# Moving one stream's layer norm to another place in a software-pipelined attention kernel, on GpSimd, VectorE, ScalarE and SyncE

## The reference

```python
def block(h, p):
    r = _retention(h, wk)                       # q k^T, causal mask, row scale, times v
    a, gate = jnp.split(r @ w1 + b1, 2, axis=-1)
    m = a * jax.nn.silu(gate) @ w2 + b2
    y = _groupnorm1(m, gg, gb) + h              # one mean and variance for a whole sequence
    f = jax.nn.gelu(y @ wf1 + bf1_, approximate=False) @ wf2 + bf2_
    return (_layernorm(f + y, lg, lb), None)    # mean and variance of each token
x = _layernorm(x + scan(block))
x = _layernorm(x + experts(x))                  # gates = entmax_bisect(x Wr + br)
```

## Time and profile before

| | |
|---|---|
| Median of 3 runs | 2443.53 us (2442.73 to 2443.81) |
| The profiled execution | 2442.89 us, of which the span of its instructions is 2441.2 |
| PE busy | 2378.8 us, 97% |
| VectorE busy | 1606.4 us, 66% |
| GpSimd busy | 1433.5 us, 59% |
| ScalarE busy | 1341.2 us, 55% |
| One step (window 644 to 709 us of the span) | 65.0 us: PE busy 62.56, VectorE 47.27, ScalarE 41.28, GpSimd 36.75 |

### The profile page before, as it was taken

How to read it: one execution, slowest core, us unless ns; L and a number is a source line. 1 busy time by engine, 2 the same in 40 slices (tenths; PEclk the granted TensorE clock), 3 DMA queues, 4 the chain that set the end, 5 groups by cost and what they waited for, 6 DMA issues and landing times. The chain is left out here.

```text
span 2441.2 us, 34911 instructions
## 1 busy us (share of the span) xinstructions
PE 2378.8 (97%) x11242; PEld 1968.7 (81%) x11242; DVE 1606.4 (66%) x2953; ACT 1341.2 (55%) x2343; POOL 1433.5 (59%) x1565
## 2 busy tenths in 40 slices
PE   9999999999999999989999999999999999999998
PEld 7888778877888888777888888888888888888886
DVE  3667767667776776678887856665646756565545
ACT  5666666666666666655655544444444444444443
POOL 2345665566655755577987955555645556554444
PEclk9999999999999999999999999999999999999999
DMA  7134454443444344436756554543445433444442
GB/s 250 44 87 103 104 143 100 104 96 99 109 99 97 87 95 100 114 103 208 238 204 211 185 210 160 186 150 137 151 178 185 160 143 138 158 160 168 151 159 74
DMA packets 354870, 344.70 MB, mean 141 GB/s; under 512 B 233872, under 2 KB 319120, under 8 KB 338320
## 3 DMA queue, kind: packets, MB, share of 16 engines
q1 hardware_dynamic: 353728, 341.85, 45.0%
q10 hardware_dynamic: 976, 0.81, 0.1%
HBM read 244.70 MB, written 97.91 MB: 140 GB/s over the span
## 5 line engine op out<-in xcount | busy, mean ns | idle before, releaser
L808 POOL TENSOR_TENSOR hid_lo<-full,hid_hi 128x512 fp32r<-128x512 f32 x384 | 505.4, 1331 | 513.7 <-ACT full L1084 462.2
L1594 DVE SCALAR_TENSOR_TENSOR full<-ps,bias_cols,sum 128x512 f32<-128x512 f32 x384 | 288.1, 750 | 215.7 <-PE ps L1872 196.6
L1870 PE MATMUL ps<-hid_hi,m_w 128*128 128x512 f32 x1024 | 401.8, 392 | 0.1
L1872 PE MATMUL ps<-hid_hi,m_w 128*128 128x512 f32 x1024 | 398.8, 389 | 0.0
L1871 PE MATMUL ps<-hid_lo,m_w 128*128 128x512 f32 x1024 | 398.5, 389 | 0.0
L1081 ACT ACTIVATE hid_hi<-ps,bias_cols 128x512 fp32r<-128x512 f32 x128 | 88.3, 690 | 495.2 <-PE ps L1872 495.2
L1870 PE MATMUL ps<-te_hi,m_w 128*128 128x512 f32 x896 | 351.1, 392 | 1.6 <-DVE sum L1581 1.0
L1872 PE MATMUL ps<-te_hi,m_w 128*128 128x512 f32 x896 | 349.0, 390 | 0.0
L1871 PE MATMUL ps<-te_lo,m_w 128*128 128x512 f32 x896 | 348.7, 389 | 0.0
L1872 PEld LDWEIGHTS ps<-hid_hi,m_w 128*128 128x128 f32 x1024 | 192.2, 188 | 40.3
L1870 PEld LDWEIGHTS ps<-hid_hi,m_w 128*128 128x128 f32 x1024 | 192.3, 188 | 39.6 <-issue 0.5
(11 more groups left out here) (209 smaller groups left out, 5576.5 us busy)
## 6 DMA issues: line engine op xcount, KB each, us to landing
m_w<-prepared SPq DMA_DIRECT2D x96, 1408.0 KB, 6.0
prepared<-m_w SPq DMA_DIRECT2D x32, 1408.0 KB, 5.8
h_store<-h_out SPq DMA_DIRECT2D x32, 512.0 KB, 3.6
we_raw<-in_W SPq DMA_DIRECT2D x64, 256.0 KB, 6.4
gate_bc<-gate_rows SPq DMA_DIRECT2D x64, 256.0 KB, 6.3
z_store<-tmp SPq DMA_DIRECT2D x120, 128.0 KB, 4.0
z<-z_store SPq DMA_DIRECT2D x30, 512.0 KB, 3.9
hT_store<-z SPq DMA_DIRECT2D x96, 128.0 KB, 3.4
```

What stands on the lines that cost most here:

```text
L808: nc.gpsimd.tensor_tensor(out=hid_lo[:, k, :], in0=full[:, k, :], in1=f32(hid_hi[:, k, :]), op=ALU.subtract).then_inc(hid_ready, 1)
L1594: nc.vector.scalar_tensor_tensor(out=full[:, k, :], in0=src, scalar=b1_col(e, 2 * fp + BLOCK_ROW[k]), in1=other[:, :], op0=ALU.add, op1=AL ...
L1870: nc.tensor.matmul(out, w[0], x[0], start=first, stop=False, skip_group_check=True)
L1872: return nc.tensor.matmul(out, w[1], x[0], start=False, stop=last, skip_group_check=True)
```

## The change

It moves steps of B's layer norm and what lies around it; no arithmetic is added or left out.

- SyncE: B's store of z is issued by chunk (store_z_chunk), four transfers of 64 KB for c = 0 and four for c = 1, each behind its own turn_z. load_T(B) goes behind load_z(B). The counts Z_STORE and Z_MOVE become one for each slot.
- GpSimd: layernorm_rstd(B, earlier) goes to the head of the body (behind the split of qk at a seam); layernorm_out(B, earlier), eight instructions in one stretch, goes from behind rstd_group(A) and the split of f2 to behind split_f(B) and layernorm_rstd(A).
- ScalarE: normalise_z(B, earlier) goes behind high_t(A), in front of the scores of A; high_t(B) goes in front of the load of the Gelu table; the high half of vm at a seam goes in front of high_u(B, 1).
- VectorE: statistics and variance of B(earlier) go to the head of the body, in front of residual(A); turn_z(A) goes into the gated products of B, turn_h(A) behind them; statistics of A go in front of its gated products; residual(B, 0) goes between gated(A, 1) and low_u(A, 1), turn_z(B, 0) behind low_t(B), residual(B, 1) between groupnorm_var(A) and groupnorm_out(A), turn_z(B, 1) behind low_p(B), turn_h(B) directly behind it; in A's groupnorm_out summed(1) comes before low_y(0).
- TensorE: group_moments of B goes behind two blocks of A's scores instead of three, group_moments of A in front of the last quarter of down_projection(B, 1).

```diff
-        Z_STORE, Z_MOVE = P // BLOCK * DMA, (P // BLOCK + 1) * DMA
+        Z_STORE = [n * (P // BLOCK) * DMA for n in (1, DC)]
+        Z_MOVE = [n + DMA for n in Z_STORE]
...
+            def store_z_chunk(s, it, c):
+                sp.wait_ge(z_ready[s], it * U + residuals(s, c) + 1)
+                for q in range(P // BLOCK):
+                    sp.dma_start(z_blocks[s, q][:, c], turned_z(s)[q * BLOCK:(q + 1) * BLOCK, c, :].rearrange("p (n b) -> p n b", b=BLOCK)
+                                 ).then_inc(z_moved[s], DMA)
...
-                store_z(B_, it - 1)
+                for c in range(DC):
+                    store_z_chunk(B_, it - 1, c)
                 if lc_of is not None:
                     load_lc(B_, lc_of)
-                load_T(B_, it + 1)
                 if earlier and turn:
                     store_hT(B_, it - 2)
                 load_z(B_, it - 1, turn)
+                load_T(B_, it + 1)
...
@@ gpsimd body
+                if earlier:
+                    layernorm_rstd(B_, earlier)
                 split_h(A_, now)
...
                     split_f(B_, before)
+                    layernorm_rstd(A_, before)
                     if earlier:
-                        layernorm_rstd(B_, earlier)
-                    layernorm_rstd(A_, before)
+                        layernorm_out(pool, nc.gpsimd, B_, earlier)
...
                     split_weight("f2", now.layer)
-                if earlier:
-                    pool.wait_ge(y_ready[A_], now.base + 2)
-                    layernorm_out(pool, nc.gpsimd, B_, earlier)
...
@@ scalar body
                     gate(B_, before, 1)
+                    if seam:
+                        next_high_weight("vm", now.layer, m_psum[B_], before)
                     high_u(B_, before, 1)
                     load_table(ACT.Gelu)
                 high_t(A_, now)
-                if seam:
-                    next_high_weight("vm", now.layer, m_psum[B_], before)
+                if earlier:
+                    normalise_z(B_, earlier)
...
+                high_t(B_, now)
                 load_table(ACT.Gelu)
-                high_t(B_, now)
                 if before:
                     normalise_z(A_, before)
...
-                if earlier:
-                    normalise_z(B_, earlier)
...
@@ vector, groupnorm_out
                 summed(0)
-                between()
                 gained(1)
-                meanwhile(0)
-                low_y(s, at, 0)
-                meanwhile(1)
-                dve.wait_ge(gn_done[s], base + 10)
-                summed(1)
+                if s == A_:
+                    dve.wait_ge(gn_done[s], base + 10)
+                    summed(1)
+                    low_y(s, at, 0)
+                else:
+                    meanwhile(0)
+                    low_y(s, at, 0)
+                    meanwhile(1)
+                    dve.wait_ge(gn_done[s], base + 10)
+                    summed(1)
                 low_y(s, at, 1)
...
@@ vector body
+                if earlier:
+                    for blocks in HALVES:
+                        layernorm_stats(B_, earlier, blocks)
+                    layernorm_var(B_, earlier)
                 if before:
                     for c in range(DC):
                         residual(A_, before, c)
-                    for c in range(DC):
-                        turn_z(A_, before, c)
+                    gated_products(B_, before, lambda c: turn_z(A_, before, c))
                     if earlier and turn:
                         turn_h(A_, earlier)
-                    gated_products(B_, before)
...
-                if earlier:
+                if before:
                     for blocks in HALVES:
-                        layernorm_stats(B_, earlier, blocks)
-                    layernorm_var(B_, earlier)
+                        layernorm_stats(A_, before, blocks)
+                    layernorm_var(A_, before)
+                gated(A_, now, 0)
+                low_u(A_, now, 0)
+                gated(A_, now, 1)
                 if before:
-                    gated_products(A_, now, lambda part: layernorm_stats(A_, before, HALVES[part]))
-                    layernorm_var(A_, before)
                     residual(B_, before, 0)
-                    turn_z(B_, before, 0)
-                else:
-                    gated_products(A_, now)
+                low_u(A_, now, 1)
...
                 if before:
+                    turn_z(B_, before, 0)
                     groupnorm_in(A_, now)
                     groupnorm_var(A_, now)
-                groupnorm_out(A_, now, between=lambda: before and residual(B_, before, 1))
+                    residual(B_, before, 1)
+                groupnorm_out(A_, now)
+                low_p(B_, now, range(TB))
                 if before:
                     turn_z(B_, before, 1)
-                low_p(B_, now, range(TB))
+                if earlier and turn:
+                    turn_h(B_, earlier)
...
@@ tensor body
-                scores(A_, now, (0, 1, 2), before)
+                scores(A_, now, (0, 1), before)
                 if before:
                     group_moments(B_, before)
-                scores(A_, now, (3,), before)
+                scores(A_, now, (2, 3), before)
...
                     out_projection(A_, now)
-                    down_projection(B_, before, 1)
+                    down_projection(B_, before, 1, (0, 1, 2))
                 group_moments(A_, now)
-                if not before:
+                if before:
+                    down_projection(B_, before, 1, (3,))
+                else:
```

More of the change, by code:

```diff
@@ L527, in store_z @@
                                  ).then_inc(z_moved[s], DMA)
+            def store_z_chunk(s, it, c):
[3 more added lines that the diff above has]
+                                 ).then_inc(z_moved[s], DMA)
             def load_z(s, it, turned=True):
-                sp.wait_ge(z_moved[s], it * Z_MOVE + Z_MOVE + Z_STORE)
+                sp.wait_ge(z_moved[s], it * Z_MOVE[s] + Z_MOVE[s] + Z_STORE[s])
                 if turned:
@@ L615, in _ @@
                 sp.sem_inc(hT_stored[s], H_STORE)
-                sp.sem_inc(z_moved[s], Z_MOVE)
+                sp.sem_inc(z_moved[s], Z_MOVE[s])
             load_part(0, 0, kq_loaded)
@@ L670, in _ @@
             store_h(B_, STEPS - 3)
-            store_z(B_, STEPS - 2)
+            for c in range(DC):
+                store_z_chunk(B_, STEPS - 2, c)
             load_z(B_, STEPS - 2, False)
@@ L1321, in gated @@
                 if c == 0:
-                    dve.wait_ge(z_moved[s], at.it * Z_MOVE + Z_STORE)
+                    dve.wait_ge(z_moved[s], at.it * Z_MOVE[s] + Z_STORE[s])
                 dve.wait_ge(m_psum[s], at.base + 2 * c + 2)
@@ L1367, in groupnorm_var, with groupnorm_out @@
                                                op0=ALU.mult, op1=ALU.subtract, reverse1=True).then_inc(g_var[s], U)
-            def groupnorm_out(s, at, meanwhile=lambda part: None, between=lambda: None):
+            def groupnorm_out(s, at, meanwhile=lambda part: None):
                 sq, mom, rstd, gain, off0, off = group_parts(s)
@@ L1422, in layernorm_stats @@
                 else:
-                    dve.wait_ge(z_moved[s], at.it * Z_MOVE + 2 * Z_MOVE)
+                    dve.wait_ge(z_moved[s], at.it * Z_MOVE[s] + 2 * Z_MOVE[s])
                 for k in blocks:
@@ L1738, in body @@
                     low_hT(A_, step_behind(dve, now))
-                if earlier and turn:
-                    turn_h(B_, earlier)
                 for half in range(2):
```

## The result

The changed kernel takes 2405.77 us (median of 4 runs, 2404.53 to 2407.02) against 2443.13 us for the kernel before beside it: 0.9848 of it, 95% interval 0.9831 to 0.9865, 37.4 us less. The forecast was 2414, its range 2396 to 2436. The profiled execution took 2406.80 us, its span is 2405.1.

The account below looks back on a forecast made before the run. TensorE, busy for 97% of the span, was taken as the bound, so only its idle time could be won. 45.6 us gross less 4 and 12 gave 29.6 off 2442.9, plus 0.6 between profiled run and median: 2414, range 2396 to 2436.

Parts of the forecast that it names:

- The sum: Whole kernel: 45.6 us gross won, less 4 for A's moments and 12 for the step's head, 29.6 net.
- That term, 2.0 each: First steps of three layers: residual wait of 2.41 us goes, stall reappears at y(A); 2.0 us won each, 6 together.
- The head: Head of the step: z(B) lands 1.8 us late, TensorE loses 1.0 us with refilling, 12 us in 12 steps.
- The moments of A: A's moments, asked for before down_projection(B, 1) ends: wait of 0 to 0.9 us, 0.3 taken for 14 steps, 4 us.
- (1): Ordinary step, B's score block 3: TensorE's 0.92 us wait for residual(B, 1) goes, 1.1 us won.
- (2): Ordinary step: TensorE's 0.80 us wait for the low half of y(A), c = 1, goes, 1.0 us won.
- (3): Ordinary step: TensorE's two 0.27 us waits for GpSimd's low halves of f(A) go, 1.1 us won.
- (a): Rival: all covers hold, z(B) and gn_in arrive in time; 2398 us, chance 0.25.
- (c): Rival: GpSimd's norm beside low_u(A) delays out_projection(A), 7 us on top, 2421 us; counted within the forecast's chance of 0.43.
- (d): Rival, head: half transfers cost whole ones, z(B) 5.5 us late, 56 us lost in 12 steps; 2458 us, chance 0.10.
- (b): Rival, head of the step: z(B) 3 us late, 2.2 us of wait in 12 steps; 2428 us, chance 0.14.
- (e): Rival: waits go but work is bound one instruction later everywhere, y_hi(A) only 0.2 us ahead; 2441 us, chance 0.08.

Follow-up runs that it names:

- e3_resid_first: The changed kernel with A's two residuals in front of B's statistics at the head of VectorE's body; 2396.0 us, ratio 0.9811.
- e1_a_order: The kernel before with only A's order changed (residual(B, 1), summed(1) and A's moments earlier), B's norm left in place; 2441.7 us, ratio 0.9998.
- e2_norm_only: The changed kernel with A's old order put back, so B's layer norm stays moved; 2426.01 us, ratio 0.9933.
- e4_whole_store: The changed kernel with B's z stored in one piece again, four transfers of 128 KB; 2423.32 us, ratio 0.9925.
- e6_seam_split: On e3_resid_first, B's norm cut in two on GpSimd in a layer's first step, bias behind A's power; 2399.0 us, ratio 0.9819.

## Why the prediction was right, and where it was not

**The sum.** 45.6 gross, 12 for the head, 4 for the moments, 29.6 net; 37.4 measured. Ordinary intervals gained 2.1 us each on average (14.6 / 7), where 3.3 less 1.0 and 0.3 is 2.0; they are 61.3 to 63.8 us long, 62.7 on average, where 62.5 to 63.3 was written. The missing part lies in the first steps of the layers: 14.0 us for the six intervals around them, where the prediction's terms give some 9 (for each interval behind a first step 2.0 less 1.0 for the head, for each one before it 3.3 less 1.3). The interval behind a first step lost 3.0 to 3.6 us, since a stall of 2.41 us for the residual fell to 1.05 for y and 1.17 for gin. That term, 2.0 each, was sized too small. Apart, the three intervals behind a first step give 9.7 us where the terms say 3.0, and the three before one 4.3 where they say 6.0.

The traces show two things that the prediction had no term for. One is a single stall in the interval into the third layer's first step, in which TensorE, VectorE and ScalarE wait for nothing that the profile names. On TensorE it has grown from 0.95 to 2.37 us, and that interval gained only 0.7 us, the others of its kind 1.7 and 1.9. What causes it stays open. The line of the kernel before, then that of the changed one:

```profile
530.93 0.49 PE L1870 MATMUL ps<-ry_sp,w_fold 128*128 128x512 f32 x1 [0.95 <-issue]
...
514.90 0.49 PE L1885 MATMUL ps<-ry_sp,w_fold 128*128 128x512 f32 x1 [2.37 <-issue]
```

The other is TensorE's clock. In the kernel before its granted clock is 0.50 (1.2 GHz instead of 2.4) for 3.4 us from 317.3, for 6.8 us from 842.9 and for 6.8 us from 1078.4; the first two stretches lie at the end of, or just behind, a wait of 2.4 us for the residual (the third such wait, at 580.80, has none). In the changed kernel it is 0.50 for 3.4 us from 516.3, just behind the stall, and for 6.8 us from 1042.0. Matmuls of 512 columns start 0.43 us apart there instead of 0.23. That is 17.0 against 10.2 us. An estimate from the spacing gives at most 3 us of the 37.4, and less where a slower TensorE meets the next wait later: the intervals behind the first steps took 66.73, 66.78 and 67.03 us in the kernel before, with 3.4, 0 and 6.8 us at the lower clock, and only the second has a wait for y's low half (1.07 us).

**The head.** "z lands at 662.7: 1.8 us late": 1.75 in the step shown and 1.35 on average. The chain from store to load was priced at 8.6 us; it takes 8.60 in the step shown and 8.0 on average, 7.6 to 8.8. 0.8 us of wait for TensorE was foreseen at out_projection(B); it is there in eight steps, 0.28 to 1.05 us. e3_resid_first gives 9 us for what was priced at 12. This step holds, a little oversized. One figure beside it is a slip: with 12.5 us from store to landing for 0.8 of wait, a wait of 3.5 needs some 15 us and not 14.4.

**The moments of A.** "A wait between 0 and 0.9, mostly once. I take 0.3 for 14 steps." Wrong in place. In ordinary steps A's moments cause no wait to speak of; nine of the 13 waits for gin are at B's moments, which the change also asks for earlier (eight of 0.16 to 0.21 us and one of 0.45), and four at A's: three of 1.0 to 1.17 us in the first steps of a layer and one of 0.23. The total, 5.5 us, is near the 4 priced, by luck.

**The waits (1), (2) and (3) as separate terms.** This is the step that failed, though it does not show in the time. The prediction added the three waits as if each could be won without the others; it named what GpSimd slows as a part of (2) and gave that no share. The expectations of e1 and e2 took it at its word, (1) and (2) for the order and (3) for the norm: 2.1 and 1.1 us a step. e1_a_order wins 1 us and not 29, e2_norm_only 17 and not 5 to 12. In its place: (2) has two sufficient cures. GpSimd's norm slowed a sum from 0.74 to 1.22 us and a subtraction from 0.69 to 1.13, and with it gone the wait goes in the old order as well; the new order alone takes it away too. And neither (1) nor (2) can be won while the norm stands between y(A) and the masks: TensorE then reaches retain(B) before GpSimd. The forecast of the whole came out since the change does both; a forecast of either half by the same sum would have been off by 28 or by 5 to 12 us. The profile had said it: the earlier trace rows shows GpSimd's norm, masks and low halves without a gap from 645.38 to 660.3, a chain that starts at y(A) and ends at a wait of TensorE, so what is saved beside it was bound to end there, as the masks of e1_a_order show (21.8 us).

**The rivals.** (a), all covers hold, 2398, is what e3_resid_first makes of the kernel (2396.0), so its price was right and its condition wrong by 1.4 us of lateness. (c), GpSimd's norm beside low_u(A), is half true: in the step shown they take 1.16 and 1.06 us instead of 0.69, but u is ready in time; there is no wait of TensorE for it in the ordinary steps, and one of 0.69 us in the last step. (d) has the right place and the wrong size: even e4_whole_store makes the head cost 27 us (9 and 18), not 56. (b), 3 us late, isn't met in the changed kernel: the latest step is 2.2 us late. (e) is out: between first steps and the last one TensorE waits for the high half of y(A) once, 0.23 us. In the first steps that wait came as foreseen, 0.9 to 1.05 us.

**A page beside it.** On GpSimd and VectorE the Trainium skill (SBUF — State Buffer, "SBUF: two separate sides") says that the shared pair of ports goes to whoever starts first, for its whole instruction, when VectorE reads two inputs in SBUF and GpSimd reads SBUF. The runs agree: L1388 with both inputs in SBUF takes 1.16 us instead of 0.75 beside GpSimd, L1383 with one of them in PSUM 0.74 either way, and an operation of two elements 0.72 instead of 0.16: 0.56 us more, within the 0.7 us of one GpSimd instruction.

## What to carry to other kernels

Waits of the bounding engine in one step must not be summed as if they were independent, as this kernel shows: follow each behind the one that would be next, and see whether a gapless chain of another engine joins them (here norm, masks, low halves). If it does, only shortening or moving the chain frees the rest, and a run with each half of the change alone tells it. A load from HBM put in front of an in-order engine's step is best placed behind the work that doesn't need it: 1.4 us of residuals in front of the statistics hid a lateness of 1.35 us and were worth 9 us.

## What the runs showed of the hardware that was not expected

The same four transfers of 128 KB to hT_store are issued in 4.70 us in the kernel before, of which one takes 2.17 and the others 0.61 to 0.65, and in 3.10 in the changed kernel and 3.60 in e4_whole_store, where none takes over 0.9; four of 64 KB mostly take 1.9 to 2.0 (2.9 in the step at 632 us, where one takes 1.50). That the backlog in front is what holds the one transfer is argued and not shown. A chain of transfers is thus priced by the durations of its own place in the queue. And VectorE's smallest operations, on two or four values, suffer most from GpSimd in proportion: 0.16 us becomes 0.72, three in a row take 0.44, 0.65 and 0.66 instead of 0.16 to 0.22 (e6_seam_split), and the one on four values behind A's statistics (L1448 of the changed kernel) takes 1.05 us at 673.18 beside a GpSimd subtraction on 128x512, where it takes 0.17 at the head.
